# A transformer block with routed experts: a new order of all steps, with 538 products of ones for 731

## What is computed

```python
x = layernorm(x + attn1(x))          # 16 heads of 8, 4 key/value heads, rope, tanh cap, causal
h = layernorm(x) * g1 + b1
x2 = x + attn2(h) @ wo + bo          # 16 heads of 8, softmax over 256 keys
h2 = layernorm(x2) * g2 + b2
idx = argmax(h2 @ gate_w + gate_b)   # one of 8 experts
moe = relu(h2 @ w1[idx] + b1[idx]) @ w2[idx] + b2[idx]
out = layernorm(x + x2 + moe)
```

## Time and profile before

| what | us |
|---|---|
| median of three runs | 636.28 |
| lowest and highest run | 631.78, 637.45 |
| span of the profiled execution, first to last instruction | 634.2 |
| first `d_max` of batch 0 starts | 75.9 |
| last `d_max` of batch 15 ends | 534.8 |

### The profile page before, as it was taken

How to read it: one execution, slowest core, us unless ns; L and a number is a source line. 1 busy time by engine, 2 the same in 40 slices (tenths; PEclk the granted TensorE clock), 3 DMA queues, 4 the chain that set the end, 5 groups by cost and what they waited for, 6 DMA issues and landing times.

```text
span 634.2 us, 17034 instructions
## 1 busy us (share of the span) xinstructions
PE 566.4 (89%) x6112; PEld 352.5 (56%) x6112; DVE 490.1 (77%) x1360; ACT 422.3 (67%) x645; POOL 417.1 (66%) x441
## 2 busy tenths in 40 slices
PE   2697789999998999999999999999999999989891
PEld 2364344555454645555555665656656566578791
DVE  1735997798987897889889989999997978455542
ACT  1384717878796687587789598969777582645560
POOL 3357947576869678577786878879766062546664
...
GB/s 142 160 2 18 1 31 41 10 2 10 25 22 18 10 10 19 21 9 10 37 10 95 51 102 23 11 2 7 54 47 113 80 54 331 72 128 153 180 148 11
DMA packets 31731, 35.98 MB, mean 57 GB/s; under 512 B 6890, under 2 KB 23696, under 8 KB 31648
## 3 DMA queue, kind: packets, MB, share of 16 engines
q1 hardware_dynamic: 27712, 27.16, 14.8%
q0 software_dynamic: 2784, 6.43, 2.8%
...
...
## 4 chain that ended last, share of the span: by engine, by line
PE 56%; DVE 18%; issue 7%; POOL 6%; ACT 6%; SPq 3%; DMA 3%; ACTq 0%; POOLq 0%; DVEq 0%
PE out L1033 8%; DVE mx L1386 7%; PE ring_p L857 7%; PE ring_s L1019 5%; PE ring_p L1099 5%; PE ring_s L999 4%; PE out L918 3%; PE ring_p L1087 3%; PE ring_s L905 2%; SPq L788 2%; PE ring_p L970 2%; PE ring_p L977 2%; DMA qs<-mT 2%; PE ring_s L1087 2%; PE out L931 2%
## 5 line engine op out<-in xcount | busy, mean ns | idle before, releaser
L1386 DVE TENSOR_REDUCE mx<-ring_s 128x4 f32<-128x1024 f32 x128 | 152.1, 1219 | 11.5 <-PE ring_s L999 9.9
L1160 ACT ACTIVATE p<-ring_s 128x1024 f32<-128x1024 f32 x128 | 125.2, 1028 | 28.2 <-PE ring_s L1019 27.6
L857 PE MATMUL ring_p<-blank 128*128 128x256 f16 x633 | 110.9, 284 | 14.9 <-DMA w_qkv<-in_L_attn_w_v 9.5
L1129 ACT ACTIVATE p<-ring_s 128x1024 f32<-128x1024 f32 x96 | 96.7, 1023 | 35.2 <-PE ring_s L905 33.6
L1590 POOL TENSOR_SCALAR stack<-stack 128x256 f16<-128x256 f16 (+1 forms) x96 | 65.6, 706 | 64.7 <-DVE stack L1378 33.2
L1587 POOL TENSOR_TENSOR rs<-ms,small 128x40 f32<-128x40 f32 x14 | 96.0, 6860 | 14.8 <-DVE ms L1249 14.4
L1606 POOL TENSOR_SCALAR_AFFINE_SELECT p<-p 128x512 f32<-128x512 f32 (+1 forms) x96 | 76.4, 805 | 36.8 <-ACT p L1133 36.1
L1133 ACT ACTIVATE p<-p 128x1024 f32<-128x1024 f32 x96 | 99.1, 1059 | 0.5
L857 PEld LDWEIGHTS ring_p<-blank 128*128 128x128 f16 x633 | 57.8, 102 | 49.5 <-issue 23.7
L1033 PE MATMUL out<-p,v 128*32 128x256 f32 x1024 | 69.1, 398 | 0.0
L999 PE MATMUL ring_s<-kc,qs 32*128 32x256 f16 x512 | 50.1, 278 | 9.0 <-DVE qs L1300 3.4
...
## 6 DMA issues: line engine op xcount, KB each, us to landing
...
qs<-mT SPq DMA_DIRECT2D x64, 2.0 KB
...
out<-t_y,t_idx POOLq DMA_INDIRECT x39, 2.8
...
```

Source lines behind the costliest of these rows:

```text
L857: nc.tensor.matmul(spare[:, 0:256], blank[:, 0:P], blank[:, 0:256], start=True, stop=True)
L1129: nc.scalar.activation(p1[:, u], bank(f"b_sc{u}", n)[:], ACT.Tanh, scale=float(ISQ / CAP)).then_inc(b_s.sem, 1)
L1160: nc.scalar.activation(p2[:, u], bank(f"e_sc{u}", n)[:], ACT.Exp, scale=float(ISQ)).then_inc(e_s.sem, 1)
L1386: nc.vector.tensor_reduce(mx2[:, t, 2 * pair:2 * pair + 2, 2 * k:2 * k + 2], bank(f"d_mx{j}", n)[:].rearrange("p (z g s) -> p z g s", z=2, ...
```

## The change

All ranks are new, in their order and not only in their numbers, and there are 538 fillers in place of 731. How many lie between which steps, counted in the two orders:

| from the start, or from this step, to the next one | before | after |
|---|---|---|
| start | 128 | 221 |
| `d_mx0(0)` | 358 | 233 |
| `d_mx0(9)` | 148 | 59 |
| `d_mx7(15)` | 68 | 22 |
| `f_rank(15)` to the end | 29 | 3 |

```diff
 ORDER = {
-    "a_load": (0, 180, 160, 3120, 3100, 7360, 10240, 13500, 16700, 19500, 22940, 25580, 28980, 31980, 36580, 39280),
...
-    "p_parts": (5580,),
...
-    "p_plan": (33520, 47440, 55600, 57920),
...
+    "a_load": (0, 37, 36, 34, 39, 268, 605, 727, 861, 962, 1203, 1252, 1446, 1744, 1850, 1845),
...
+    "d_max0": (366, 530, 663, 814, 968, 1108, 1241, 1383, 1524, 1691, 1871, 2012, 2115, 2296, 2431, 2546),
...
+    "p_parts": (154,),
+    "p_plan": (1672, 2274, 2644, 2732),
...
+    "w_fill": (1, 2, 3, 4, 5, 6, 7, 8, 9, 10, 11, 12, 13, 14, 15, 16, 17, 18, 19, 20, 21, 22, 25, 26, 27, 28, 29, 30,
...
             def g_row(s):
                 k = plan_of(s)
                 sp.wait_ge(r_v.sem, r_v.upto(k, "row"))
-                for n in scattered[s][-2:]:
+                for n in (PLANS[k][0] - 1, PLANS[k][0]):
                     wait_turn(sp, rows_out[n % 2], n, 2, 16 * T)
                 if s == PLANS[k][1]:
                     if k >= LAST:
```

More of the change, by code:

```diff
@@ L176 @@
[L176 to L186, removed]
-    "b_sc0": (940, 1860, 4500, 7860, 11020, 14200, 16440, 19280, 22580, 26560, 30160, 33380, 37540, 39460, 42620,
-        45880),
@@ new lines @@
+    "a_pow": (235, 355, 492, 664, 798, 942, 1096, 1223, 1377, 1525, 1673, 1800, 1992, 2093),
+    "a_qT": (131, 178, 324, 434, 576, 721, 863, 1002, 1171, 1326, 1452, 1613, 1775, 1903, 2050, 2193),
+    "a_qTc": (134, 197, 327, 450, 578, 741, 875, 1021, 1174, 1330, 1463, 1617, 1779, 1906, 2056, 2197),
+    "a_qkv": (33, 82, 200, 329, 464, 632, 766, 912, 1057, 1204, 1354, 1497, 1638, 1778, 1950, 2064),
+    "a_root": (77, 135),
+    "a_rope": (35, 84, 213, 339, 469, 643, 782, 923, 1069, 1209, 1357, 1501, 1649, 1782, 1961, 2069),
@@ new lines @@
+    "a_split": (83, 147, 271, 396, 520, 694, 825, 972, 1129, 1301, 1405, 1582, 1747, 1852, 2025, 2138),
+    "a_stack": (85, 156, 274, 417, 526, 709, 835, 979, 1150, 1310, 1415, 1589, 1754, 1886, 2030, 2156),
+    "a_sum": (38, 86, 219, 344, 471, 654, 787, 933, 1086, 1213, 1370, 1518, 1654, 1790, 1969, 2075),
+    "a_xT": (23, 76, 151, 215, 364, 598, 697, 805, 971, 1166, 1236, 1371, 1541, 1758, 1882, 2008),
+    "a_xTc": (24, 78, 181, 217, 391, 599, 701, 855, 973, 1172, 1302, 1380, 1578, 1760, 1887, 2014),
[24 rows of a table added]
@@ new lines @@
+    "c_mo": (267, 382, 512, 728, 862, 981, 1119, 1258, 1447, 1575, 1739, 1846, 1982, 2163, 2310, 2459),
+    "c_o": (246, 354, 494, 700, 804, 940, 1079, 1231, 1378, 1548, 1662, 1808, 1958, 2106, 2253, 2408),
+    "c_oT": (255, 358, 500, 707, 826, 948, 1089, 1235, 1400, 1558, 1666, 1817, 1964, 2117, 2264, 2432),
+    "c_oTc": (256, 365, 501, 708, 850, 951, 1091, 1240, 1432, 1560, 1690, 1827, 1966, 2121, 2275, 2436),
+    "c_ob": (244, 343, 489, 659, 794, 937, 1073, 1225, 1361, 1513, 1659, 1784, 1954, 2087, 2247, 2406),
@@ new lines @@
+    "c_pow": (270, 397, 519, 740, 873, 992, 1130, 1264, 1455, 1584, 1763, 1853, 1987, 2172, 2319, 2464),
[4 rows of a table added]
+    "c_r": (265, 374, 508, 725, 857, 960, 1099, 1249, 1441, 1570, 1736, 1843, 1978, 2147, 2303, 2447),
+    "c_sum": (222, 338, 466, 642, 783, 924, 1067, 1214, 1355, 1503, 1655, 1769, 1949, 2066, 2239, 2399),
+    "c_x1": (330, 446, 692, 785, 909, 1078, 1255, 1336, 1484, 1729, 1785, 1943, 2059, 2259, 2414, 2584),
+    "c_xh": (273, 416, 524, 748, 884, 1017, 1154, 1309, 1460, 1587, 1767, 1866, 2007, 2179, 2351, 2478),
@@ new lines @@
+    "c_y": (264, 369, 505, 716, 854, 954, 1094, 1247, 1436, 1564, 1732, 1838, 1971, 2136, 2292, 2439),
+    "d_b0": (322, 432, 575, 762, 908, 1053, 1189, 1325, 1480, 1623, 1799, 1935, 2051, 2214, 2380, 2494),
+    "d_b1": (328, 433, 588, 765, 911, 1058, 1195, 1339, 1483, 1627, 1802, 1947, 2061, 2218, 2383, 2502),
+    "d_hi": (331, 436, 593, 769, 913, 1063, 1198, 1343, 1488, 1634, 1810, 1951, 2063, 2221, 2393, 2506),
+    "d_kT": (353, 504, 624, 799, 946, 1087, 1221, 1365, 1509, 1656, 1857, 2002, 2095, 2260, 2420, 2529),
@@ new lines @@
+    "d_kTc": (360, 510, 631, 808, 949, 1101, 1234, 1376, 1512, 1665, 1864, 2005, 2104, 2265, 2424, 2535),
+    "d_lo": (334, 470, 597, 771, 915, 1066, 1202, 1347, 1490, 1639, 1824, 1953, 2067, 2233, 2395, 2509),
+    "d_m": (467, 596, 747, 899, 1050, 1191, 1303, 1450, 1579, 1774, 1939, 2110, 2230, 2377, 2484, 2605),
+    "d_mT": (463, 589, 743, 894, 1046, 1182, 1298, 1444, 1571, 1768, 1932, 2105, 2222, 2372, 2479, 2600),
+    "d_mTc": (465, 591, 745, 896, 1048, 1187, 1300, 1449, 1577, 1770, 1936, 2107, 2226, 2374, 2481, 2602),
[16 rows of a table added]
@@ new lines @@
+    "d_nm": (451, 586, 739, 883, 1043, 1179, 1289, 1439, 1568, 1766, 1929, 2099, 2220, 2370, 2476, 2598),
+    "d_qT": (350, 495, 619, 788, 932, 1085, 1218, 1364, 1507, 1653, 1848, 1975, 2082, 2255, 2415, 2523),
+    "d_qTc": (357, 517, 627, 801, 957, 1103, 1228, 1366, 1515, 1668, 1860, 1993, 2089, 2262, 2419, 2526),
+    "d_qkv0": (319, 429, 554, 758, 904, 1047, 1185, 1322, 1476, 1616, 1781, 1925, 2046, 2208, 2373, 2491),
+    "d_qkv1": (326, 431, 583, 760, 907, 1052, 1192, 1332, 1479, 1620, 1793, 1941, 2055, 2212, 2379, 2497),
@@ new lines @@
+    "d_stack": (341, 472, 601, 777, 920, 1070, 1207, 1352, 1496, 1644, 1831, 1959, 2071, 2237, 2405, 2513),
+    "d_xT": (316, 421, 538, 753, 900, 1023, 1159, 1317, 1467, 1606, 1773, 1918, 2028, 2188, 2358, 2485),
+    "d_xTc": (318, 422, 545, 755, 903, 1028, 1162, 1320, 1469, 1608, 1777, 1919, 2032, 2195, 2365, 2488),
[16 rows of a table added]
+    "f_gate": (644, 793, 941, 1071, 1220, 1348, 1489, 1632, 1816, 1984, 2146, 2251, 2398, 2516, 2625, 2715),
+    "f_hT": (637, 781, 934, 1059, 1210, 1340, 1474, 1624, 1795, 1977, 2139, 2246, 2389, 2507, 2614, 2705),
@@ new lines @@
+    "f_hTc": (639, 789, 936, 1064, 1217, 1344, 1477, 1628, 1807, 1980, 2142, 2249, 2392, 2510, 2615, 2708),
+    "f_ln": (623, 778, 919, 1055, 1206, 1334, 1468, 1619, 1786, 1944, 2133, 2241, 2381, 2496, 2612, 2698),
+    "f_mo": (602, 751, 901, 1045, 1184, 1318, 1457, 1609, 1776, 1930, 2112, 2229, 2371, 2489, 2603, 2690),
+    "f_o": (558, 717, 844, 1007, 1163, 1290, 1430, 1572, 1718, 1891, 2057, 2202, 2344, 2475, 2588, 2675),
+    "f_oT": (577, 722, 865, 1013, 1169, 1304, 1434, 1583, 1730, 1898, 2070, 2211, 2352, 2477, 2590, 2677),
@@ new lines @@
+    "f_r": (590, 746, 898, 1034, 1181, 1312, 1454, 1607, 1771, 1927, 2097, 2223, 2368, 2487, 2599, 2687),
+    "f_rank": (661, 802, 950, 1090, 1229, 1360, 1500, 1641, 1837, 1995, 2155, 2266, 2411, 2527, 2637, 2723),
+    "f_res": (633, 831, 974, 1161, 1269, 1401, 1470, 1618, 1783, 1972, 2191, 2273, 2390, 2499, 2635, 2730),
+    "f_scatter": (843, 1006, 1019, 1170, 1285, 1505, 1566, 1652, 1915, 2178, 2245, 2281, 2524, 2567, 2648, 2733),
+    "f_sum": (552, 711, 834, 993, 1142, 1271, 1394, 1535, 1695, 1884, 2047, 2194, 2327, 2469, 2576, 2667),
@@ new lines @@
+    "f_y": (585, 738, 877, 1027, 1177, 1308, 1448, 1605, 1748, 1913, 2092, 2216, 2359, 2483, 2596, 2683),
+    "g_down": (1806, 1822, 1997, 2023, 2129, 2204, 2231, 2240, 2317, 2474, 2508, 2534, 2543, 2608, 2610, 2654, 2674,
+        2720, 2729, 2739, 2748, 2763, 2775, 2785, 2796, 2806, 2819, 2827, 2839, 2850, 2862, 2871, 2883, 2895, 2905,
+        2915, 2924, 2932, 2941),
+    "g_hT": (1726, 1731, 1815, 1869, 2035, 2040, 2113, 2175, 2268, 2430, 2434, 2486, 2505, 2539, 2549, 2601, 2606,
+        2679, 2685, 2718, 2724, 2737, 2743, 2766, 2770, 2780, 2790, 2804, 2811, 2826, 2838, 2844, 2855, 2870, 2882,
+        2888, 2899, 2914, 2919),
@@ new lines @@
+    "g_hTc": (1728, 1735, 1818, 1896, 2037, 2043, 2123, 2183, 2289, 2433, 2438, 2490, 2511, 2542, 2580, 2604, 2607,
+        2681, 2688, 2721, 2726, 2740, 2747, 2768, 2773, 2783, 2793, 2808, 2817, 2829, 2841, 2849, 2860, 2873, 2884,
+        2894, 2903, 2916, 2922),
+    "g_mid": (1753, 1762, 1911, 2009, 2085, 2116, 2171, 2232, 2298, 2453, 2473, 2498, 2522, 2586, 2592, 2651, 2660,
+        2692, 2696, 2731, 2735, 2757, 2761, 2777, 2787, 2797, 2810, 2820, 2832, 2842, 2853, 2863, 2876, 2887, 2896,
+        2907, 2918, 2927, 2933),
@@ new lines @@
+    "g_out": (2086, 2079, 2150, 2217, 2299, 2295, 2467, 2396, 2536, 2577, 2611, 2640, 2626, 2697, 2666, 2738, 2717,
+        2753, 2771, 2779, 2764, 2788, 2802, 2813, 2821, 2848, 2837, 2857, 2867, 2878, 2889, 2900, 2910, 2917, 2928,
+        2935, 2942, 2947, 2949),
+    "g_row": (1689, 1701, 1716, 1798, 1787, 1794, 1861, 1694, 1955, 2332, 2324, 2342, 2397, 2417, 2309, 2321, 2437,
+        2664, 2668, 2699, 2706, 2694, 2684, 2755, 2760, 2765, 2769, 2789, 2778, 2805, 2823, 2812, 2828, 2859, 2840,
+        2874, 2881, 2893, 2909),
@@ new lines @@
+    "g_rs": (1897, 1904, 2048, 2140, 2166, 2224, 2279, 2316, 2329, 2495, 2520, 2547, 2564, 2618, 2633, 2663, 2707,
+        2728, 2744, 2750, 2759, 2776, 2795, 2798, 2809, 2825, 2830, 2843, 2854, 2865, 2875, 2885, 2897, 2908, 2923,
+        2925, 2934, 2944, 2945),
+    "g_up": (1750, 1751, 1905, 2004, 2078, 2111, 2148, 2225, 2293, 2445, 2470, 2492, 2517, 2582, 2587, 2630, 2643,
```

(24 more changed lines are left out.)

273 lines of the change are left out of this document (7 added, 266 removed), and 134 rows, old and new, of the table ORDER.

## The result

The changed kernel takes 638.68 us, median of 20 runs (635.48 to 643.31), beside 634.47 for the kernel before (631.78 to 637.45): ratio 1.0066, 95% interval 1.0042 to 1.0090. It is a little slower, where 617 was forecast. Its profiled execution has a span of 635.2 us (own time 636.95), 1.0 us longer than before's.

What follows compares the result with a forecast made beforehand. TensorE was taken as full because filled, with fillers partly on the path. From 634.2 us, less 3.3 (start), less 19.7 (fillers), plus 3.6 (clock) gave a 614.8 span; 2.1 more for the median made 616.9, written 617; range 597 to 640.

Steps and rivals of the forecast that it cites:

- the fillers after the start: Taking fillers out of the four stretches after the start gains 19.7 us, by their chain share; upper bound 31.5.
- The second rival: Fillers stood in real waits, where TensorE now waits; only the start's 3.3 us are left: 634 us, chance 0.17.
- the rest of the order: Every engine's list reshuffled by a few places: taken as nothing, allowing 5 us of gain or 10 of loss.
- the fourth rival: An order that stalls an engine behind an unready step: within the 10 us allowed, its chance counted with the second rival.
- The clock: Fewer fillers in the middle leave more waits: one more fall to half clock, 3.6 us lost; range none to three.
- The third rival: Slower by the clock: e_sc stages without fillers each let it fall; ten falls give 649 us, chance 0.13.
- The start: Up to the first row maxima: 3.3 us less, from 5 less to 3 more, p_parts and added fillers together.
- Its largest term: p_parts moved behind a_split(1) on VectorE, so the first row maximum comes earlier: gain 6.5 us, between 2 and 6.5.
- the cover: VectorE's room at 29 to 41 us, busy 1.0 of 12, for p_parts; if gone, at most 6.5 us again.
- the added fillers: More fillers at the start, as 22 instead of 6 ahead of a_xT(0): 3.2 us later, between 1.5 and 5.
- Loads: a_load(3) goes ahead of a_load(1), one more issue of some 0.5 us behind 36 fillers: nothing.
- the waits of `g_row`: In SyncE's queue, g_row(8) no longer waits for batch 10's scatter: nothing, between 0 and 1 us of gain.

Runs made afterwards that it cites:

- experiment 3: The kernel before, its order kept, with the fillers after d_mx0(0) thinned evenly to the changed kernel's numbers: 643.95 us, ratio 1.0118.
- experiment 5: The kernel before with its order and all 731 fillers, those after the first 128 half as wide: 637.10 us, ratio 1.0029.
- experiment 6: The changed kernel with slot 13's weights fetched early and every filler of the middle issued twice, 584 for 292: 638.74 us, ratio 1.0075.
- experiment 1: The changed kernel with slot 13's weights, g_w(13), fetched ahead of q_pad0 instead of behind q_pad5: 629.52 us, ratio 0.9865.
- 2: The kernel before with slot 13's weights, g_w(13), moved behind q_pad5: 651.38 us, ratio 1.0261.
- 8: The changed kernel with slot 13's weights early and at most six fillers in a gap of the start, 68 for 221: 631.00 us, ratio 0.9927.
- 7: The kernel before with p_parts moved behind a_split(1): 635.83 us; with batch 1's residual and moments also behind batch 0's first two row maxima: 638.15 us.
- 9: The kernel before with only the new waits of the row fetches, on the scatters of batches 6 and 7: 634.92 us, ratio 1.0005.

## Why the prediction was wrong, by its steps

The measured 638.68 lies inside the range of 597 to 640, near its upper end and on the other side of the kernel before than the forecast.

**The step that failed on the sum: the fillers after the start, 19.7 us.** The prediction took their share of the chain of waits as what taking them out gives, in proportion to their number. The fillers did leave the chain, and in the middle (first `d_max` of batch 0 to that of batch 15) TensorE stood still 19 us more, 39.1 for 20.2, but the middle grew from 446.7 to 450.9 us at about the same clock. In the old order the same thinning made the kernel slower (experiment 3), and fillers of half the time gave back at most a sixth of what they saved (5); in the new one, fillers put in cost about a quarter of what the chain says (6). The chain names one path; the sum needed how much shorter the next one is, through `d_max` and `e_exp`, which is where the rows of after went. VectorE was named as what is late next, and dismissed at 90% of the two long stretches; it has 86% of them, 402.8 of 469.7 us. The second rival said that only the start would be left, at 634, and its band of 630 to 642 holds the measured time; but that is luck in part, since without the late fetch it is 629.52. It rested in part on the Trainium skill's "Perfetto Trace Analysis", section "Identifying the Most-Contended Engine": by that rule, taking out fillers gives nothing. Experiment 5 agrees (27.0 us less of filler time, and a middle 0.3 us longer); experiment 6 doesn't wholly, TensorE has no room for 292 more without the 8.0 us.

**The step that failed on the sign: "the rest of the order", nothing, with 10 us for a loss.** The bound was about right and the place was missed. I followed SyncE's queue for `a_load`, `g_row` and `d_m`, but not for `g_w`, and so did not see one fetch go behind six writes of 660 KB with the last batch's row maxima queued behind its user. It cost 7 to 13 us in the new order (1) and 17 in the old one (2), and is the fourth rival: an order that stalls an engine.

**The clock.** One more fall, 3.6 us. In the middle there is none more (half clock 20 us for 22, by the rows); the stall of `g_up(13)` made one. (Of the two slices in the earlier trace rows that were to show what goes ahead of a fall, the second, with 1.26 us, holds the fall itself: its clock is 0.75.) The third rival, slower by the clock, was right about the old order thinned (643.95), but the new order with as few fillers holds its clock: 0.97 and 0.99.

**The start.** 3.3 us forecast; measured 6.2 in the changed kernel's profile (69.7 us for the 72.6 named) and 1.2 to 1.6 in four others of the same start (8). Its largest term was wrong: in the old order `p_parts` alone gives 0.6, not 6.5 (7). The prediction named the cover, and priced its loss at up to 6.5 us again; that end was the one. For the added fillers 3.2 us later had been forecast: the profile with 68 of them is about 4 us ahead of four with 221 and 0.8 behind one, by where a fall of the clock lies, so that this term is not settled. Which steps of the new start make the gain together is not settled.

**Loads, the waits of `g_row`.** The waits at nothing: right (9). The loads were not tried by themselves.

**The sum, mended** from the two profiles: the start -6.2 us, the middle +4.2, batch 15's row maxima +6.6, what stands behind them -3.7, together about the 1.0 us; forecast were -3.3, -14.3, 0 and -5.4, and 3.6 more for the clock. The ratio says 4.2 us in place of 1.0; the later start of the other four profiles would add up to 5 us, but which start the runs without a profile had is not known. Why the new order's middle, at the same clock and with fewer fillers, is 4 us longer than the old one's is open: the waits are spread over all batches, and no run took single steps back. By the price that experiment 6 gives (8.0 us for 292), 214 fillers fewer would be worth some 6 us, and the rest of the new order would then cost some 10 us in the middle besides the fetch; that is an estimate which no run tests.

**The better version** is experiment 1, faster than the kernel before by 0.75% by medians (629.52 for 634.31) and 1.35% by the ratio.
